# Layer norm powers in five groups instead of four, and a plan of fractional due times with some twenty of its numbers changed

## What is computed

```python
xn = layernorm(x)                                   # x: 8 x 512 x 128
q, k, v = xn@Wq+bq, xn@Wk+bk, xn@Wv+bv               # 8 heads of 16
attn = softmax(q k^T / 4)
out1, out2 = attn @ [v1, v1], attn @ [v2, v2]        # halves of the heads
s = ((1-0.8) * layernorm(out1 - lam*out2)*ln_w+ln_b) @ Wo + bo
h = mod(int(xn[:, 0] + xn[:, 1]), 8); experts h and h+1 of 8, weight 1/2 each
ffn = sum_e w_e * (relu(xn @ W1_e + b1_e) @ W2_e + b2_e)
return x + s * silu(ffn)
```

## Time and profile before

| | us |
|---|---|
| median of 3 runs | 422.58 (422.43 to 423.55) |
| the profiled execution | 423.16 |
| its span, first to last instruction | 421.3 |
| PE busy in the span | 389.6 (92%) |
| DVE busy | 300.1 (71%) |
| ACT busy | 268.5 (64%) |
| POOL busy | 153.2 (36%) |

### The profile page before, as it was taken

One profiled execution on the slowest core, in us unless ns is written; L12 is line 12 of the kernel. 1 busy time (PEld: TensorE's weight loads), 2 busy tenths in 40 slices (PEclk: granted clock), 3 DMA queues, 4 the chain that ended last, 5 costly groups with the idle time before them and its releaser, 6 DMA issues.

```text
span 421.3 us, 8389 instructions
## 1 busy us (share of the span) xinstructions
PE 389.6 (92%) x2575; PEld 249.2 (59%) x2576; DVE 300.1 (71%) x793; ACT 268.5 (64%) x667; POOL 153.2 (36%) x188
## 2 busy tenths in 40 slices
PE   4986979999999999999999999999999999999984
PEld 1343868655676657666665668666666657663322
DVE  6797886667687766866676768766686767766884
ACT  3571556666667765577765767576665668575783
POOL 7753302172235442374335421642353232420100
PEclk9997799999999999999999999999999999999997
DMA  7974763244305640235504540344255141214840
GB/s 243 343 226 116 196 217 90 75 112 140 133 13 167 197 143 14 77 109 160 186 16 130 173 137 18 128 137 157 61 163 172 25 161 49 78 19 127 299 165 25
DMA packets 36946, 54.76 MB, mean 130 GB/s; under 512 B 6724, under 2 KB 25141, under 8 KB 36903
## 3 DMA queue, kind: packets, MB, share of 16 engines
q1 hardware_dynamic: 31456, 46.94, 33.5%
q0 software_dynamic: 3296, 6.76, 7.6%
q10 hardware_dynamic: 2151, 0.53, 0.6%
HBM read 15.59 MB, written 6.75 MB: 53 GB/s over the span
## 4 chain that ended last, share of the span: by engine, by line
PE 76%; DVE 11%; ACT 4%; issue 4%; DMA 2%; POOL 2%; DVEq 0%; ACTq 0%; POOLq 0%
PE ring L1383 14%; PE ring L1404 14%; PE pv_bank L1317 13%; PE score L1279 13%; PE exp L1304 11%; DVE neg_max L1034 4%; PE ring L1241 2%; PE ring L1343 2%; PE ring L1266 2%; PE ring L1325 1%; ACT hT L813 1%; ACT xin L775 1%; DMA qs<-max_rows 1%; DMA xs<-xn_rows,inverse 1%; PE ring L1365 1%
## 5 line engine op out<-in xcount | busy, mean ns | idle before, releaser
L1034 DVE TENSOR_REDUCE neg_max<-score 128x1 f32<-128x512 f32 x256 | 170.7, 685 | 70.2 <-PE score L1279 65.3
L1279 PE MATMUL score<-ks,qs 96*128 96x512 bf16 x256 | 98.4, 388 | 8.6 <-DVE neg_max L1034 7.4
L775 ACT ACTIVATE xin<-exp 128x512 f32<-128x512 f32 x120 | 70.1, 604 | 39.0 <-PE exp L1304 36.2
L1304 PE MATMUL exp<-qs,ks 99*128 99x512 bf16 x244 | 91.8, 380 | 3.2 <-ACT xin L775 1.5
L813 ACT ACTIVATE hT<-ring,pair 128x128 f32<-128x128 f32 x256 | 73.5, 375 | 28.1 <-PE ring L1383 25.4
L775 ACT ACTIVATE probs<-exp 128x512 f32<-128x512 f32 x124 | 72.8, 611 | 28.3 <-PE exp L1304 26.9
L679 POOL DMA_INDIRECT y_rows<-y_sb,inverse x32 | 32.0, 999 | 137.8 <-DVE y_sb L1166 136.6
L1404 PEld LDWEIGHTS ring<-w_sb,hT 128*128 128x128 f32 x568 | 74.2, 193 | 8.7 <-issue 2.1
L1404 PE MATMUL ring<-w_sb,hT 128*128 (+1 forms) x568 | 76.4, 278 | 0.8 <-ACT hT L813 0.8
L1383 PEld LDWEIGHTS ring<-xsT,pair 128*128 128x128 f32 x512 | 65.1, 191 | 13.8 <-issue 7.9
L1383 PE MATMUL ring<-xsT,pair 128*128 128x128 f32 x512 | 69.4, 278 | 0.5 <-issue 0.5
(11 more groups left out here) (195 smaller groups left out, 409.3 us busy)
## 6 DMA issues: line engine op xcount, KB each, us to landing
pair<-table SPq DMA_DIRECT2D x32, 580.0 KB
qs<-parts SPq DMA_DIRECT2D x42, 128.0 KB
ks<-parts SPq DMA_DIRECT2D x42, 128.0 KB
xin<-_attn_hidden_states_dram SPq DMA_DIRECT2D x8, 256.0 KB, 5.5
table<-in_L_ffn_W_dram SPq DMA_DIRECT2D x2, 1024.0 KB, 9.8
w_sb<-in_L_ffn_W_dram SPq DMA_DIRECT2D x8, 256.0 KB, 6.1
xn_rows<-xn SPq DMA_DIRECT2D x8, 256.0 KB, 3.1
table<-_attn_hidden_states_dram SPq DMA_DIRECT2D x8, 256.0 KB, 4.7
```

The lines of the kernel that those rows point to most:

```text
L775: a.activation(prob(n), exp_banks[n][:, :], ACT.Exp, scale=SCALE).then_inc(exp_done, 1)
L1034: v.tensor_reduce(neg_max[:, b % 2, col:col + 1], score_bank[n % 2][:, :], AX.X, ALU.max, negate=True).then_inc(max_taken, 1)
L1279: t.matmul(score_bank[n % 2][:, :], qs[0:MAX_ROW, b % STK, hh, c * P:(c + 1) * P], ks[0:MAX_ROW, b % STK, hh, :], start=True, stop=True).t ...
L1304: t.matmul(exp_banks[n][:, :], ks[0:KROWS, b % STK, hh, kc * P:(kc + 1) * P], qs[0:KROWS, b % STK, hh, :], start=True, stop=True).then_inc ...
```

## The change

Three things change. **Powers:** LN_GROUPS has five groups, and for all but the last POOL also makes `shift` itself (minus the mean, then times rstd), so that DVE has no `shift` step for them. **Count:** the sum of the first two values is formed from raw x, ahead of the wait for the last power; then it is multiplied by rstd, and twice the shift is added. **Plan:** constants move by 0.05 to 1.5 units.

```diff
-LN_GROUPS = ((0, 1), (1, 3), (3, 6), (6, 8))
+LN_GROUPS = ((0, 1), (1, 2), (2, 4), (4, 6), (6, 8))
-SHIFT_AT = (-58.5, -56.5, -51.5, -50)
+SHIFT_AT = (-58.5, -57.5, -55.5, -53.5, -50)
-EXTRAS_AT = 5.7
-GROUPS_AT = (9.05, 11.05, 13.05, 14.05)
+EXTRAS_AT = 5.2
+GROUPS_AT = (9.05, 10.72, 13.05, 14.05)
-FFN_FIRST = 8.4
-EXTRA_PACE = 2.6
-STATIC_FIRST = 27.6
+FFN_FIRST = 7.6
+EXTRA_PACE = 2.3
+STATIC_FIRST = 27.33
-INIT_AHEAD = 1
-H1, D0, D1 = 1.5, 3.3, 4.5
+INIT_AHEAD = 1.5
+H1, D0, D1 = 1.8, 3.3, 4.5
-SPLIT_MAX, TURN_MAX = 16.6, 19.3
-EXP_OFF, PV_OFF = 0.2, 3.5
-NORM_O, TURN_Z, PROJECT_O = 42.6, 41.5, 45.5
-LAMBDA_AT = 19
-FOLD_AT = 21
-TANH, GATE = 0.7, 1.7
+SPLIT_MAX, TURN_MAX = 16.8, 18.9
+EXP_OFF, PV_OFF = 0.05, 4
+NORM_O, TURN_Z, PROJECT_O = 41.76, 40.67, 45.16
+LAMBDA_AT = 18.67
+FOLD_AT = 20.5
+TANH, GATE = 0.7, 1.84
...
-                at(qkv + 5 + 4 * i, "split", b, i)
-        at(32 * b + LAG - 27.8 if b else FOLD_AT + 6.2, "values", b)
+                at(qkv + 5.4 + 4 * i, "split", b, i)
+        at(32 * b + LAG - 28.3 if b else FOLD_AT + 6.2, "values", b)
...
-            at(16 * grp + LAG + 20, "copy_o", grp)
-            at(16 * grp + LAG + 22.2, "turn_o", grp)
+            at(16 * grp + LAG + 19.17, "copy_o", grp)
+            at(16 * grp + LAG + 22.03, "turn_o", grp)
...
-        at(t - 6, "load_x", f)
+        at(t - 6.66, "load_x", f)
...
                     pool.wait_ge(stats_ready, end)
+                    if end < B:
+                        g.tensor_scalar(shift[:, tok], mv[:, tok, 0], -1.0, None, ALU.mult)
...
+                    if end < B:
+                        pool.wait_ge(rstd_ready, s[1] + 1)
+                        g.tensor_tensor(shift[:, tok], shift[:, tok], rstd[:, tok], ALU.mult).then_inc(shift_ready, 1)
...
-                link(v.tensor_tensor(two, xin[:, :, 0:2], rstd[:, :].unsqueeze(2).to_broadcast([P, NT, 2]), ALU.mult))
-                link(v.tensor_tensor(two, two, shift[:, :].unsqueeze(2).to_broadcast([P, NT, 2]), ALU.add))
-                link(v.tensor_tensor(v01[:, :], two[:, :, 0], two[:, :, 1], ALU.add))
+                dve.wait_ge(pair_summed, 1)
+                link(v.tensor_tensor(v01[:, :], v01[:, :], rstd[:, :], ALU.mult))
+                dve.wait_ge(shift_ready, len(LN_GROUPS))
+                link(v.scalar_tensor_tensor(v01[:, :], shift[:, :], 2.0, v01[:, :], ALU.mult, ALU.add))
...
+                    v.tensor_tensor(v01[:, :], xin[:, :, 0], xin[:, :, 1], ALU.add).then_inc(pair_summed, 1)
```

More of the change, by code:

```diff
@@ L74 @@
 PAIR_AT = (20, 21, 22)
-INIT_AHEAD = 1
-H1, D0, D1 = 1.5, 3.3, 4.5
+INIT_AHEAD = 1.5
+H1, D0, D1 = 1.8, 3.3, 4.5
 TT = 2
-SPLIT_MAX, TURN_MAX = 16.6, 19.3
-EXP_OFF, PV_OFF = 0.2, 3.5
-NORM_O, TURN_Z, PROJECT_O = 42.6, 41.5, 45.5
-LAMBDA_AT = 19
-FOLD_AT = 21
-TANH, GATE = 0.7, 1.7
+SPLIT_MAX, TURN_MAX = 16.8, 18.9
[4 more added lines that the diff above has]
+TANH, GATE = 0.7, 1.84
 GATE_SCALE = 0.25
-LOAD_Y_AT = 249
+LOAD_Y_AT = 250.2
 FINISH_AT = (258.7, 260, 261, 264, 266, 268, 272.5)
@@ L381, in gated_attention_moe @@
         shift_ready = sem("shift_ready")
+        pair_summed = sem("pair_summed")
         b1_loaded = sem("b1_loaded")
@@ L876, in count_groups @@
                 dve.wait_ge(iota_ready, 1)
-                two = cmp[:, 0:2 * NT].rearrange("p (t k) -> p t k", k=2)
-                link(v.tensor_tensor(two, xin[:, :, 0:2], rstd[:, :].unsqueeze(2).to_broadcast([P, NT, 2]), ALU.mult))
-                link(v.tensor_tensor(two, two, shift[:, :].unsqueeze(2).to_broadcast([P, NT, 2]), ALU.add))
-                link(v.tensor_tensor(v01[:, :], two[:, :, 0], two[:, :, 1], ALU.add))
+                dve.wait_ge(pair_summed, 1)
+                link(v.tensor_tensor(v01[:, :], v01[:, :], rstd[:, :], ALU.mult))
+                dve.wait_ge(shift_ready, len(LN_GROUPS))
+                link(v.scalar_tensor_tensor(v01[:, :], shift[:, :], 2.0, v01[:, :], ALU.mult, ALU.add))
                 link(v.scalar_tensor_tensor(v_abs[:, :], v01[:, :], -1.0, v01[:, :], ALU.mult, ALU.max))
@@ L1000, in _ @@
                     first, end = LN_GROUPS[g]
+                    if end < B:
+                        continue
                     tok = slice(C * first, C * end)
+                    v.tensor_tensor(v01[:, :], xin[:, :, 0], xin[:, :, 1], ALU.add).then_inc(pair_summed, 1)
                     dve.wait_ge(rstd_ready, g + 1)
```

## The result

| | before | after |
|---|---|---|
| median, us | 422.50 (421.05 to 423.55, 4 runs) | 412.15 (410.43 to 413.44, 4 runs) |
| ratio to before, with 95% interval | | 0.9749 (0.9724 to 0.9775) |
| the profiled execution | 423.16 | 410.43 |
| its span | 421.3 | 408.5 |

The forecast was 419.6 us in a range from 416.6 to 423.2. The change brought 10.4 us where 3.0 were forecast, and lies outside the range. The median before is 422.50 with a fourth run beside the three that stood at 422.58.

The account below looks back on a forecast made before the run. The prediction took PE's sum of products to bound the long middle and a string of dependent work the start. Terms of -1.2 (front), -0.8 (extra tiles), -1.0 (middle) and 0 (end) sum to -3.0: 422.58 to 419.6 us, range 416.6 to 423.2.

Parts of the forecast that it names:

- The bound of the middle: From 60 to 400 us the sum of PE's products is the time; reordering can save at most the 9.5 us idle.
- rival C: More than forecast: extra tiles give 3 us, front 1.7, middle 2; -6.7 in all, 415.9 us; chance 0.20.
- The triples of scores: Middle: PE waits for maxima where three scores stand nearly together; seven such places become five, -1.2 us.
- I count nothing for them: Middle: later value products and moved gathers and DMAs of the maxima were priced at 0, with 1 us either way.
- Rival B: Slower: in 13 groups the maxima's transpose ahead of value products makes PE wait for DVE's split; 426.1 us, chance 0.11.
- 0.3 us or more: Sign against the forecast: L1294 shows up among PE's waits with 0.3 us or more each.
- The front: Start: statistics without stops, earlier last power and shorter head of the count bring the first gather 1.2 us earlier.
- The copy on ACT that was to hold the peel: Start: ACT normalizes batch 2 until 23.14, so the projection's first copy, at 23.93, gains only 0.8 us.
- the rule of the exclusive lock: Start: by this port rule the pair sum would wait for POOL's 1.67 us power, and the head give 0.1, not 0.4.
- The extra tiles: Between 32 and 60 us: the new order wins back a fifth of 4.2 us of PE's idle time, -0.8 us.
- The stretch at 0.50: Lower clock from 36-37 to 46-47 us; nothing shortens it; each us there is worth half a us of products.
- The tail: End: order of the last scores, split, value products and output is unchanged; 0, within 0.3 us.

Follow-up runs that it names:

- a_noo5: The changed kernel with NORM_O, TURN_Z, PROJECT_O, copy_o and turn_o put back to their old values; ratio 0.9852 to the kernel before, middle 313.67 us.
- b_warm: The kernel before plus 14 spare products whose result nobody reads, six behind scores, eight ahead of the first extra tile's transpose; ratio 0.9952, 2.0 us of median.
- b_extras: The kernel before with only the new plan of the extra tiles; ratio 0.9966 to the kernel before, 1.4 us.
- m_os: The kernel before with new front, extra tiles' plan, outputs' group and static tiles' timing, rest of the middle old; ratio 0.9870, middle 315.44 us.
- m_osm: The kernel before with new front, extra tiles' plan, outputs' group, static tiles' timing and maxima; ratio 0.9790, middle 312.11 us.
- m_oxs: The kernel before with new front, extra tiles' plan, outputs' group, static tiles' timing, exponentials and value products; ratio 0.9805, middle 312.04 us.
- a_nomax: The changed kernel with SPLIT_MAX 16.6 and TURN_MAX 19.3 back, so the maxima's transpose stands behind the value products; ratio 0.9824, middle 311.38 us.
- a_warm: The changed kernel plus the 14 spare products in the same places, behind the first six scores and ahead of the first extra tile's transpose; ratio 0.9745.

## Why the prediction was wrong

**The bound of the middle: the step that failed.** The text said that PE is busy 330.46 of 340, "so no reordering can take out more than what PE idles there", and it looked for gains only among the waits that the profile lists. Three quarters of the middle's gain were in time that this view calls busy: short losses under the end of the product before (-2.5), 0.16 at each of six idle places fewer (-1.0), and entries into value products (-1.2). Read by starts, the old middle had about 20 us to lose (22 with the pace of the v projections), not the seven or so that it idled. The bound alone would still have left room for 6 us, since PE idled 9.5; it made the text look at listed waits only, and of these it priced the triples and put all the rest at nothing, "with 1 us either way". That is why the range ended at 416.6, and rival C at 415.9.

**The triples of scores: right, and only a part.** Seven triples to five was to bring -1.2. The listed waits for neg_max in the middle went from 4.2 us in 10 to 3.0 in 8, and the scores named, 34, 41, 82 and 178, waited 0.44, 0.71, 0.52 and 0.51 us. "I count nothing for them" (value products, gathers, DMAs of the maxima) was wrong: the waits of exponentials for ACT went from 2.0 to 1.0, and the transposes of the maxima, which the text treated only as a danger, took away 13 entries. Against that, 1.5 us of listed waits are new (for a gather, for xsT, and "issue" ahead of L1392 0.3 longer).

**Rival B's condition did not come.** The splits ended 0.26 to 1.92 us ahead of the thirteen transposes that stand before value products. The one wait of L1294 for the split, 0.33 us, is in the last group, which the change had left alone; by the letter it is the sign of "0.3 us or more" that the text had set, once and not "each". That such a transpose can do harm is shown by a_noo5, through the ring.

**The front: right, and the -2.0 of the table is partly luck.** Statistics without a stop (-1.47 forecast), last power at 16.99 (16.7), `v_abs` 1.6 earlier (1.7 to 1.8), `inverse` at 30.73 (31.1), first gather at 31.22 (31.6). The term was -1.2 and measures -1.6 at `inverse` in this pair of profiles. The first transpose came another 0.4 earlier because its gather took 4.4 us instead of 4.8; of seventeen kernels with the new front it is the earliest, and their median, 36.48, is 1.1 ahead of the old front's, 37.62. The copy on ACT that was to hold the peel (it "can come only to there") started at 22.87 by the trace of after. The pair sum took 0.20, not 0.34, and stood 0.5 us ahead of the last power. So it does not test the rule of the exclusive lock that the prediction weighed; nothing here waited for it.

**The extra tiles: -0.8 was small.** The new order alone is worth 1.0 to 2.0 us (the comparisons at equal clock above), which is a quarter to a half of the 4.2 and not a fifth. The stretch at 0.50 was to stay at 10 us and was 3.4; by b_warm the whole of it costs 2.0 us of median, where the text gave half a us for each of its 10. How much of its length is the change's doing isn't settled: of the 17 kernels with new powers, new extra tiles or both and no spare products, 13 show about 7 us, three about 3 and one about 10, in one profile each.

**The tail** lost 1.0 where nothing was forecast. I did not isolate it. With the outputs' group undone it stays at 36.6, so it is not that; and b_extras, with the old constants there, has 36.72 where the other four with the old middle have 37.27 to 37.78, so one pair of profiles can't tell 1.0 from nothing.

**Still open** is which of the plan's constants inside the static tiles' group matters, and why either of two partners does: from m_os, m_osm gains 1.3 us by entries (41 to 27), 1.1 by idle places and 0.8 by short losses, and m_oxs 2.2 by idle places (23 to 20) and 1.3 by short losses with no entry fewer, and both end at 312. That two different sets of losses give the same sum speaks for many small places and against one mechanism; it was not tested place by place. None of the other kernels is faster than the changed one beyond the intervals.

## What to carry to other kernels

Measure an in-order TensorE stream by the distances between starts, not by its busy time or its listed waits: a middle that reads 98% busy still held 6% of loss, almost a third of it recoverable by order alone. Constants of a plan act together; undoing four of the five groups one at a time, or adding the outputs alone, showed nothing here where three together bring 5 us, so search them jointly and keep the set. Put matrix instructions that cost an entry (here value products and transposes of the maxima) directly behind each other, if what they read is ready; alone it need not show in the time (a_nomax).

## What the runs showed that was not expected

- An exponential or score is recorded 0.38 us long and followed at 0.22; so a loss in front of the next is shown 0.16 short, and one of 0.24 (95.48 to 95.94) has no wait beside it.
- Value products and bf16 transposes of the maxima start 0.09 us later than other products after an exponential (0.31 against 0.22) or a tile's product (0.20 against 0.11). A value product behind such a transpose does not pay it again.
- 14 spare products in an idle stretch kept the granted clock at 1.00 from 36 to 47 us, where it had a mean of about half before, and made the kernel 2.0 us faster. In the changed kernel the same products removed the low stretch of 3.4 us and showed no gain within 2 us.
- The new head's DVE operations on 32 columns took 0.19 to 0.20 us, where the pair sum's counterpart before had taken 0.34; the cause is not shown.
- The first gather differs from kernel to kernel by nearly as much as the front gained: the transpose that waits for it starts 4.4 us after its issue in the changed kernel and 5.5 in a_noo5 and a_warm.
